# Attention passes of a two-layer transformer kernel: pieces of other work in the odd half sub-steps alone, two together

## The chip, the cores and the metric

One core of a Trainium2 chip. The metric is device microseconds of one execution; three runs of the kernel before are given. TensorE (PE) multiplies, VectorE (DVE), ScalarE (ACT) and GpSimd (POOL) do the rest, SyncE (SP) issues the DMAs. Each engine works through its own instructions in order, and waits on semaphores that others raise.

## The reference

For 4 batches of 512 tokens of 256 numbers (two layers, each an attention and a feed-forward part, each followed by a layer norm):

```python
x = L0_attn_hidden_states                         # (4, 512, 256)
x = _layernorm(x + _L0_attn_ref(x, ...))          # linear attention, 16 heads of 128, elu + 1
x = _layernorm(x + _L0_ffn_ref(x, ...))           # 8 low-rank updates, the one with the largest gate is taken
x = _layernorm(x + _L1_attn_ref(x, ...))          # below
x = _layernorm(x + _L1_ffn_ref(x, ...))           # 8 experts, the best 2, gated, plus a low-rank part

def _L1_attn_ref(x, Wq, Wk, Wv, Wo, bo):          # 16 heads of 16
    ...
    logits = jnp.einsum('bhqd,bhkd->bhqk', q, k) / jnp.sqrt(jnp.float32(hd))
    weights = jax.nn.softmax(logits, axis=-1)
    ctx = jnp.einsum('bhqk,bhkd->bhqd', weights, v)
    ctx = jnp.transpose(ctx, (0, 1, 3, 2)).reshape(B, T, D)
    return ctx @ Wo + bo
```

## The kernel before, in words

The first layer's attention runs first (some 350 us, untouched). Then come four passes over the batches, b = 0 to 3: pass b does the softmax attention of batch b, and in between it pieces of the other parts of neighbouring batches: for b+1 the update of layer 0's feed-forward part (`update`), its norm, the transposes `turn_x2`, `query_key` and `value`; for b+2 `turn_x1`, `select` and the gate's selection (`gate_...`); for b-1 `out_project`, its norm, `turn_x3`, `route`, the experts (`expert_up`, `expert_gate`, `turn_hidden`); for b-2 `expert_out` and the last norm. `more` is b+1 < 4, `most` b+2 < 4, `back` b > 0, `back2` b > 1.

A pass has 16 sub-steps (a group of 4 heads by a tile of 128 keys), each in two half steps, n = 0 to 31. In each half step, called step n from here on, TensorE does a *pair*: two transposed scores (`turned_score`, L1179, into bank_st) and, on other rows of the array, two plain scores of eight sub-steps ahead (`score`, L1158, into bank_s). ScalarE turns each transposed score into probabilities (`exponentials`, L1505), VectorE takes the maximum over the keys of each plain score (`maxima`, L1759). bank_s and bank_st have two buffers each. In even steps TensorE adds the *context* of the sub-step before (`context`, L1192, 8 matmuls into bank_c). Behind that it issues a piece of other work. The order on each engine is written out by hand: the lists of `if n == ...` in the three functions `body(b)` of TensorE (L1300), ScalarE (L1539) and VectorE (L1865). Nothing but semaphores ties the three lists together.

Two waits matter most:

```python
def score(b, h, t):
    u = 4 * h + t
    at_least(pe, max_ready, 64 * b + u - 1)      # the maximum of the score before last
def turned_score(b, s, j):
    at_least(pe, p_ready, 64 * b + u - 1)        # the exponential of the one before last
```

A third is on the banks of the pieces: side0 and side1 take the halves i = 0 and 1 of nearly all of them, and `take(i)` waits until what was last in the bank has been read (`last_read`), for example by `add_update` (L1741) after `update`, by `x2T_rest` (L1746) after `turn_x2`, by `qk_rest` (L1751) after `query_key`, by `add_attention` (L1786) after `out_project`. `query_key` waits besides for both halves of x2T_lo, `turn_x3` for x normalized by ScalarE (L1457).

The transposes of the context (`turn_context`, L1200) and of the maxima (`turn_max`, L1165), `route` and `turn_logits` go through a bank of their own, bank_t.

Of the kernel before, what the change touches and what calls it, by code (L numbers as in the profile page):

```python
# [17 lines left out]
B, T, D = 4, 512, 256  # L18
# [748 lines left out]
def update_attention_experts(nc, a, kept, out, first):  # L767
# [6 lines left out]
    with ExitStack() as ctx:  # L774
# [119 lines left out]
        def expert_half(b):  # L894

            return 20 if b + 1 < B else 16
# [167 lines left out]
        def _(pe):  # L1064
# [235 lines left out]
            def body(b):  # L1300
                more, most, back, back2 = b + 1 < B, b + 2 < B, b > 0, b > 1
                e = expert_half(b)
                for n in range(2 * SUBS):
# [18 lines left out]
                    if n in (12, 13) and more:  # L1322
                        value(b + 1, n - 12)
                    if n in (14, 15) and more:
                        query_key(b + 1, n - 12)
                    if n in (16, 17) and most:
                        turn_x1(b + 2, n - 16)
                    if n in (18, 19) and most:
                        select(b + 2, n - 18)
# [6 lines left out]
                    if n in (e + 9, e + 10, e + 11) and back:  # L1336
                        turn_hidden(b - 1, n - e - 9)
                    if n in (28, 29) and not more:
                        expert_out(b - 1, n - 28)
# [3 lines left out]
                    if n == 4:  # L1343
                        turn_max(b, 1)
# [4 lines left out]
                    if n == 13 and back:  # L1349
                        route(b - 1)  # L1350
                    if n == 14 and back:
                        turn_logits(b - 1)
# [99 lines left out]
        def _(act):  # L1452
# [86 lines left out]
            def body(b):  # L1539
                more, most, back, back2 = b + 1 < B, b + 2 < B, b > 0, b > 1  # L1540
                e = expert_half(b)
                for n in range(2 * SUBS):
# [15 lines left out]
                    if n in (10, 11) and back:  # L1558
                        x3T_out(b - 1, n - 10)
                    if n in (11, 19):  # L1560
                        shift_out(b, n // 8 + 1)
                    if n in (12, 13) and more:
                        value_out(b + 1, n - 12)
                    if n == 13 and back:
                        lgT_out(b - 1)
                    if n in (14, 15) and more:
                        qk_out(b + 1, n - 12)
                    if n in (16, 17) and most:
                        x1T_out(b + 2, n - 16)
                    if n == (16 if more else 15) and back:  # L1570
                        route_exp(b - 1)
                    if n in (17, 18) and most:
                        squares(b + 2, (0, 1) if n == 17 else (2, 3))
                    if n in (20, 21) and back2:
                        normalize(4, b - 2, xk[:, b % 2], (0, 1) if n == 20 else (2, 3))
                    if n in (e + 1, e + 3, e + 5, e + 7) and back:
# [7 lines left out]
                    if n in (e + 9, e + 10, e + 11) and back:  # L1584
                        hidden_out(b - 1, n - e - 9)
# [62 lines left out]
        def _(dve):  # L1648
# [216 lines left out]
            def body(b):  # L1865
                more, most, back, back2 = b + 1 < B, b + 2 < B, b > 0, b > 1
                e = expert_half(b)
                for n in range(2 * SUBS):
# [17 lines left out]
                    if b == 0 and n in (5, 28):  # L1886
                        residual_stats(2 + n // 28, range(NT))
                    if b == 0 and n in (6, 29):
                        residual_merge(2 + n // 29)
# [11 lines left out]
                    if n in (11, 12) and back:  # L1901
                        x3T_rest(b - 1, n - 11)
                    if n in (11, 12) and back2:
                        expert_stats(b - 2, n - 11)
                    if n in (13, 14) and most:
                        normalize_x1(b + 2, (0, 1) if n == 13 else (2, 3))
# [270 lines left out]
```

## Time and profile before

| | |
|---|---|
| median of 3 runs (757.58 to 768.87) | 761.38 us |
| the profiled execution | 755.98 us |
| its span | 754.1 us |
| TensorE busy | 701.9 us (93%) |
| VectorE busy | 506.9 us (67%) |
| ScalarE busy | 405.1 us (54%) |
| GpSimd busy | 108.6 us (14%) |
| chain that ended last | PE 71%, DVE 17%, ACT 4%, issue 4%, DMA 2% |
| maxima (L1759), 256 | 164.5 us busy, idle before them 58.5 |
| exponentials (L1505), 256 | 139.2 us busy, idle before them 66.5 |

Times in the rows are from the start of the span. A row is a group of instructions with its busy time; in brackets stands the idle time before it and what ended it. Matmuls overlap, so a busy TensorE may still be waiting in part: the length of a stretch tells more than its busy share. A row of a stretch reads: from:to, its length in us, then for each of PE, PEld (the weight loads of TensorE), DVE, ACT and POOL the busy us with the number of instructions, then the granted TensorE clock (1.00 is 2.4 GHz, 0.50 is 1.2 GHz, between them a mean over both), the DMA share and GB/s. The passes begin at 379.3, 457.5, 541.2 and 624.9 us.

### The profile page before, as it was taken

How to read it: one execution, taken by the hardware profiler on the slowest of the kernel's cores; microseconds unless marked ns; L12 is line 12 of the kernel's file. 1: busy time of each engine (PE TensorE's matmuls, PEld its weight loads, DVE VectorE, ACT ScalarE, POOL GpSimd, SP SyncE). 2: the span in 40 equal slices, each digit the busy share in tenths (PEclk: the TensorE clock that was granted, in tenths of full speed). 3: DMA queues.
4: the chain of work that ended last, by engine and by line, in shares of the span. 5: the costliest groups of instructions: out<-in, count | busy, mean ns of one | idle time of the engine just before them, and what ended most of it. 6: DMA issues, size and time to landing. Idle time of an engine off the chain costs nothing.

```text
span 754.1 us, 11354 instructions
## 1 busy us (share of the span) xinstructions
PE 701.9 (93%) x4038; PEld 481.4 (64%) x4038; DVE 506.9 (67%) x1129; ACT 405.1 (54%) x746; POOL 108.6 (14%) x107
## 2 busy tenths in 40 slices
PE   8899999999999999997899988999999999999685
PEld 5678987798779887895344634555455455355364
DVE  4566556765577566856767697969878885862351
ACT  5475356644664466443036764866656664656411
POOL 0302320132013421343001000200001000000100
PEclk9999999999999999998559999999999999899867
DMA  8300000010000020008604810373007700000000
GB/s 336 139 1 1 29 1 2 0 46 0 0 0 11 0 80 1 3 14 97 97 2 58 96 20 1 46 90 36 3 1 85 86 30 1 3 2 28 29 1 28
DMA packets 13996, 28.30 MB, mean 38 GB/s; under 512 B 2612, under 2 KB 3452, under 8 KB 13820
## 3 DMA queue, kind: packets, MB, share of 16 engines
q1 hardware_dynamic: 13948, 27.68, 19.9%
q8 instruction: 28, 0.46, 0.3%
q14 instruction: 20, 0.16, 0.1%
HBM read 12.60 MB, written 2.10 MB: 19 GB/s over the span
## 4 chain that ended last, share of the span: by engine, by line
PE 71%; DVE 17%; ACT 4%; issue 4%; DMA 2%; POOL 1%; SPq 0%; DVEq 0%; ACTq 0%; POOLq 0%
PE bank_y L414 11%; PE bank_q L355 10%; PE bank_st L1179 8%; DVE nmax L1759 7%; PE bank_c L1192 6%; PE bank_a L297 5%; PE side L1127 3%; PE bank_a L385 3%; PE side L1251 3%; PE bank_s L1158 3%; PE side L1282 2%; PE bank_a L331 2%; PE bank_n L370 2%; PE bank_q L397 2%; PE side L1211 2%
## 5 line engine op out<-in xcount | busy, mean ns | idle before, releaser
L1759 DVE TENSOR_REDUCE nmax<-bank_s 128x1 f32<-128x512 f32 x256 | 164.5, 685 | 58.5 <-PE bank_s L1158 57.3
L1505 ACT ACTIVATE shared<-bank_st 128x512 f32<-128x512 f32 x256 | 139.2, 596 | 66.5 <-PE bank_st L1179 65.8
L1158 PE MATMUL bank_s<-ks,qs 48*128 48x512 f32 x256 | 114.7, 509 | 7.9 <-DVE nmax L1759 6.2
L1179 PE MATMUL bank_st<-qs,ks 50*128 50x512 f32 x256 | 102.1, 469 | 4.3 <-ACT shared L1505 4.1
L615 DVE SCALAR_TENSOR_TENSOR sq<-bank_q,bq,eq 128x512 f32<-128x512 f32 x64 | 47.5, 744 | 47.8 <-ACT eq L498 47.8
L414 PE MATMUL bank_y<-m_hi,s_lo 128*128 128x256 f32 x256 | 73.2, 286 | 3.2 <-POOL s_lo L249 3.1
L1192 PE MATMUL bank_c<-shared,v 128*32 128x512 f32 x512 | 73.0, 644 | 0.9 <-ACT shared L1505 0.9
L1179 PEld LDWEIGHTS bank_st<-qs,ks 50*128 50x128 f32 x256 | 41.5, 192 | 50.4 <-issue 23.9
L414 PE MATMUL bank_y<-m_hi,s_hi 128*128 128x256 f32 x256 | 72.1, 282 | 0.0
L414 PE MATMUL bank_y<-m_lo,s_hi 128*128 128x256 f32 x256 | 72.1, 282 | 0.0
L249 POOL TENSOR_TENSOR s_lo<-sq,s_hi 128x512 fp32r<-128x512 f32 x32 | 42.8, 1337 | 187.2 <-ACT s_hi L503 187.2
L1158 PEld LDWEIGHTS bank_s<-ks,qs 48*128 48x128 f32 x256 | 46.2, 202 | 29.9 <-DVE nmax L1759 27.9
L503 ACT ACTIVATE s_hi<-sq 128x512 fp32r<-128x512 f32 x64 | 40.3, 631 | 44.2 <-DVE sq L632 44.2
L496 ACT ACTIVATE eq<-bank_q,bq_neg 128x512 f32<-128x512 f32 x64 | 43.8, 685 | 28.9 <-PE bank_q L355 28.1
L632 DVE TENSOR_TENSOR sq<-sq,bank_q 128x512 f32<-128x512 f32 x64 | 43.4, 684 | 23.4 <-PE bank_q L397 23.2
L355 PE MATMUL bank_q<-xT_hi,wq_lo 128*128 128x512 f32 x128 | 54.7, 428 | 3.8 <-DVE wq_lo L587 2.5
L414 PEld LDWEIGHTS bank_y<-m_hi,s_lo 128*128 128x128 f32 x256 | 48.2, 188 | 5.9 <-issue 3.5
L355 PE MATMUL bank_q<-xT_hi,wq_hi 128*128 128x512 f32 x128 | 50.5, 394 | 0.0
L355 PE MATMUL bank_q<-xT_lo,wq_hi 128*128 128x512 f32 x128 | 50.4, 394 | 0.0
L1002 POOL TENSOR_TENSOR ln_rstd<-ln_var,half 128x4 f32<-128x4 f32 x12 | 12.1, 1011 | 264.6 <-DVE ln_var L119 264.6
L414 PEld LDWEIGHTS bank_y<-m_lo,s_hi 128*128 128x128 f32 x256 | 48.2, 188 | 0.2
L414 PEld LDWEIGHTS bank_y<-m_hi,s_hi 128*128 128x128 f32 x256 | 48.2, 188 | 0.0
(264 smaller groups left out, 1330.3 us busy)
## 6 DMA issues: line engine op xcount, KB each, us to landing
qs<-qk_hi SPq DMA_DIRECT2D x16, 256.0 KB, 5.6
ks<-qk_hi SPq DMA_DIRECT2D x16, 256.0 KB, 10.3
xT<-in_xT SPq DMA_DIRECT2D x4, 512.0 KB, 4.7
sq<-in_wqT SPq DMA_DIRECT2D x2, 1024.0 KB, 9.4
wo<-in_woT SPq DMA_DIRECT2D x1, 2048.0 KB, 13.3
xs<-in_x SPq DMA_DIRECT2D x1, 2048.0 KB, 18.1
qs<-qk_lo SPq DMA_DIRECT2D x8, 256.0 KB, 7.8
ks<-qk_lo SPq DMA_DIRECT2D x8, 256.0 KB, 11.0
```

The lines of the kernel that those rows point to most:

```text
L249: pool.tensor_tensor(s_lo[:, n % 3, :], sq[:, n, :], s_hi[:, n % 3, :].bitcast(F32), ALU.subtract).then_inc(s_lo_ready[1], 1)
L355: mm = pe.matmul(q_bank("query", n)[:, :], lhs, rhs, start=i == 0, stop=i == 3 * KD - 1)
L414: mm = pe.matmul(bank_y4[:, t, :], lhs, rhs, start=n == 0 and i == 0 and t % 2 == 0, stop=n == H0 - 1 and i == 2, skip_group_check=True)
L496: act.activation(eq[:, n % 3, :], q_bank("query", n)[:, :], ACT.Relu, bias=bq_neg[:, h:h + 1], scale=-1.0).then_inc(eq_capped, 1)
L503: act.activation(s_hi[:, n % 3, :], sq[:, n, :], ACT.Copy).then_inc(s_hi_ready, 1)
L615: dve.scalar_tensor_tensor(out=sq[:, n, :], in0=q_bank("query", n)[:, :], scalar=bq1[:, h:h + 1], in1=eq[:, n % 3, :], op0=ALU.add, op1=AL ...
L632: dve.tensor_tensor(sq[:, n, :], sq[:, n, :], q_bank("factor", n)[:, :], ALU.mult).then_inc(scaled, 1)
L1158: pe.matmul(bank_s[u % 2][:, :], qs[part, b % 2, slot, t * P:(t + 1) * P], ks[part, b % 2, slot, :], start=True, stop=True).then_inc(s_don ...
L1179: pe.matmul(bank_st[u % 2][:, :], ks[part, b % 2, slot, kt * P:(kt + 1) * P], qs[part, b % 2, slot, :], start=True, stop=True).then_inc(st ...
L1192: mm = pe.matmul(bank_c[32 * j:32 * j + 32, :], v[:, b % 2, kt, 4 * g + j, :], probs[:, (4 * s + j) % SLOTS, :], start=kt == 0, stop=kt == 3)
L1505: act.activation(probs[:, u % SLOTS, :], bank_st[u % 2][:, :], ACT.Exp, scale=SCALE1).then_inc(p_ready, 1)
L1759: dve.tensor_reduce(nmax[:, g, t, j:j + 1], bank_s[u % 2][:, :], AX.X, ALU.max, negate=True).then_inc(max_ready, 1)
```

## The change

On TensorE every piece of an even step goes to the odd step after it, so that the two halves of a piece (i = 0 and 1) are issued one behind the other there; the even steps keep the pair and the context. `route` and `turn_logits` go one step later (14 and 15), the experts begin one step later (21, or 17 in the last pass), each tile's `expert_up` and `expert_gate` together in one odd step. On ScalarE and VectorE the parts that belong to the pieces follow: on VectorE mostly both halves together in the even step after. No operation is added or left out; only the order changes. The core of the diff (`e` is `expert_half(b)`):

```diff
-            return 20 if b + 1 < B else 16
+            return 21 if b + 1 < B else 17
@@ TensorE, body(b)
-                    if n < 2 and more:
-                        update(b + 1, n)
-                    if n in (2, 3) and back2:
-                        expert_out(b - 2, n - 2)
-                    if n in (4, 5) and back:
-                        out_project(b - 1, n - 4)
-                    if n in (6, 7) and more:
-                        turn_x2(b + 1, n - 6)
-                    if n in (8, 9) and more:
-                        query_key(b + 1, n - 8)
-                    if n in (10, 11) and back:
-                        turn_x3(b - 1, n - 10)
-                    if n in (12, 13) and more:
-                        value(b + 1, n - 12)
+                    if n == 1 and more:
+                        for i in range(2):
+                            update(b + 1, i)
+                    if n == 3 and back2:
+                        for i in range(2):
+                            expert_out(b - 2, i)
+                    if n == 5 and back:
+                        for i in range(2):
+                            out_project(b - 1, i)
+                    if n == 7 and more:
+                        for i in range(2):
+                            turn_x2(b + 1, i)
+                    if n == 9 and more:
+                        for i in range(2):
+                            query_key(b + 1, i)
...
                     if n in (e, e + 2, e + 4, e + 6) and back:
                         expert_up(b - 1, (n - e) // 2)
-                    if n in (e + 1, e + 3, e + 5, e + 7) and back:
                         expert_gate(b - 1, (n - e) // 2)
+                    if n == e + 8 and back:
+                        turn_hidden(b - 1, 0)
+                        turn_hidden(b - 1, 1)
+                    if n == e + 10 and back:
+                        turn_hidden(b - 1, 2)
...
-                    if n == 4:
+                    if n == (3 if b else 4):
                         turn_max(b, 1)
@@ ScalarE, body(b)
-                    if n in (6, 7) and more:
-                        x2T_out(b + 1, n - 6)
-                    if n in (8, 9) and more:
-                        qk_out(b + 1, n - 8)
+                    if n in (7, 8) and more:
+                        x2T_out(b + 1, n - 7)
+                    if n in (9, 10) and more:
+                        qk_out(b + 1, n - 9)
...
-                    if n == 9 and back:
+                    if n == 10 and back:
                         normalize(3, b - 1, xk[:, (b - 1) % 2])
@@ VectorE, body(b)
-                    if n in (1, 2) and more:
-                        add_update(b + 1, n - 1)
-                    if n in (3, 4) and back2:
-                        add_experts(b - 2, n - 3)
-                    if n in (3, 4) and more:
-                        update_stats(b + 1, (0, 1) if n == 3 else (2, 3))
-                    if n == 4 and more:
+                    if n == 2 and more:
+                        add_update(b + 1, 0)
+                        add_update(b + 1, 1)
+                    if n == 3 and more:
+                        update_stats(b + 1, range(NT))
                         merge(2, b + 1)
-                    if n in (5, 6) and back:
-                        add_attention(b - 1, n - 5)
+                    if n == 4 and back2:
+                        add_experts(b - 2, 0)
+                        add_experts(b - 2, 1)
+                    if n == 6 and back:
+                        add_attention(b - 1, 0)
+                        add_attention(b - 1, 1)
                     if n in (6, 7) and back:
                         attention_stats(b - 1, n - 6)
-                    if n == 7 and more:
+                    if n == 7 and back:
+                        merge(3, b - 1)
+                    if n == 8 and more:
                         x2T_rest(b + 1, 0)
                         x2T_rest(b + 1, 1)
-                    if n == 8 and back:
-                        merge(3, b - 1)
-                    if n in (9, 10) and more:
-                        qk_rest(b + 1, n - 9)
+                    if n == 10 and more:
+                        qk_rest(b + 1, 0)
+                        qk_rest(b + 1, 1)
...
-                    if n in (15, 16) and more:
-                        qk_rest(b + 1, n - 13)
-                    if n == 15 and back:
+                    if n == 16 and back:
                         route_rel(b - 1)
+                    if n == 16 and more:
+                        qk_rest(b + 1, 2)
+                        qk_rest(b + 1, 3)
                     if n == 16:
                         split_maxima(b, 3)
-                    if n == (17 if more else 16) and back:
+                    if n == 17 and back:
                         route_scores(b - 1)
-                    if n == (18 if more else 16) and back:
                         route_first(b - 1)
-                    if n == (19 if more else 16) and back:
+                    if n == (19 if more else 17) and back:
                         route_less(b - 1)
-                    if n == (20 if more else 17) and back:
                         route_second(b - 1)
...
                     if n in (e + 1, e + 3, e + 5, e + 7) and back:
                         weighted_up(b - 1, (n - e) // 2)
-                    if n in (e + 2, e + 4, e + 6, e + 8) and back:
-                        hidden(b - 1, (n - e) // 2 - 1)
+                        hidden(b - 1, (n - e) // 2)
```

Left out of it by the same pattern: TensorE's `turn_x3` (11), `value` (13), `query_key` 2 and 3 (15), `turn_x1` (17), `select` (19), `expert_out` of the last pass (29); ScalarE's `x3T_out` (11, 12), `value_out` (13, 14), `qk_out` 2 and 3 (15, 16), `tanh` (e, e+2, ...), `hidden_out` (e+9 and e+10); VectorE's `x3T_rest` (12), `expert_stats` (11), `normalize_x1` (13), `projections` (20), the gate's distances and inverse (21).

## Rows read from the trace of the kernel before

**Rows 1.** Stretches, passes 1 and 2 (columns: see the profile before).

```profile
457.54:541.15 83.61, 79.40 (x479) 43.58 (x479) 70.69 (x183) 53.61 (x111) 5.84 (x9) 1.00 0.33 39
541.15:624.89 83.74, 81.48 (x475) 44.78 (x475) 68.57 (x171) 52.72 (x104) 6.01 (x7) 1.00 0.35 46
```

**Rows 2.** Chain of work that ended last, pass 2: start, us, what.

```profile
548.05 2.79 PE side L1282 x12
...
555.94 1.93 PE side L1211 x8
...
567.07 1.60 PE side L1127 x6
...
600.30 0.91 PE side L1251 x6
...
601.87 1.25 PE side L1251 x6
```

**Rows 3.** Stretches as in rows 1: steps 6, 7 and 8 of pass 3.

```profile
643.05:644.72 1.67, 1.67 (x15) 0.46 (x14) 1.10 (x2) 1.07 (x2) 0.00 (x0) 1.00 0.01 4
644.72:645.99 1.27, 0.75 (x9) 0.46 (x5) 1.27 (x4) 0.76 (x3) 0.00 (x0) 1.00 0.00 0
645.99:649.77 3.78, 3.31 (x12) 0.72 (x12) 3.71 (x12) 1.53 (x3) 0.00 (x0) 0.73 0.00 0
```

**Rows 4.** Timeline, VectorE, pass 2, steps 6 to 8: start, us, engine, line, operation.

```profile
561.39 1.29 DVE L1759 TENSOR_REDUCE nmax<-bank_s 128x1 f32<-128x512 f32 x2 [0.70 <-PE bank_s L1158]
562.60 0.68 DVE L1786 TENSOR_TENSOR xk<-side,xs 128x512 f32<-128x512 f32 x1
563.19 0.74 DVE L1717 BATCH_NORM_STATS2 ln_bn<-xk 128x6 f32<-128x256 f32 x2
563.86 1.27 DVE L1759 TENSOR_REDUCE nmax<-bank_s 128x1 f32<-128x512 f32 x2
...
568.09 0.15 DVE L115 TENSOR_TENSOR ln_tmp<-ln_bn 128x4 f32<-128x4 f32 x1
...
568.62 0.17 DVE L119 SCALAR_TENSOR_TENSOR ln_var<-ln_tmp 128x4 f32<-128x4 f32 x1
```

**Rows 5.** Timeline, TensorE, pass 2, step 8: the start of query_key.

```profile
567.07 0.47 PE L1127 MATMUL side<-x2T_hi,wqkv_lo 128*128 128x512 f32 x1 [0.41 <-DVE x2T_lo L1746]
```

**Rows 6.** Timeline, VectorE, pass 1, steps 2 and 3.

```profile
464.59 0.25 DVE L1775 RECIPROCAL rsum<-bank_t 128x16 f32<-128x16 f32 x1
...
465.40 0.86 DVE L1741 SCALAR_TENSOR_TENSOR xf<-xf,keep,side 128x256 f32<-128x256 f32 x2
466.18 1.28 DVE L1759 TENSOR_REDUCE nmax<-bank_s 128x1 f32<-128x512 f32 x2
```

**Rows 7.** Stretches: 1/2-5, 2/6-15, 2/16-21, 1/16-21, 1/22-27, 0/0-7 (pass/steps).

```profile
462.81:473.89 11.08, 9.78 (x53) 5.12 (x53) 9.57 (x27) 5.84 (x12) 1.21 (x2) 1.00 0.01 2
560.82:589.83 29.01, 28.14 (x169) 15.50 (x168) 23.14 (x53) 19.36 (x39) 4.79 (x5) 1.00 0.52 64
589.83:603.04 13.21, 12.40 (x69) 5.75 (x68) 12.55 (x41) 9.46 (x19) 0.00 (x0) 1.00 0.95 103
502.91:516.98 14.07, 13.50 (x95) 7.76 (x94) 13.34 (x43) 10.60 (x26) 0.00 (x0) 1.00 0.89 96
516.98:532.55 15.57, 14.81 (x95) 8.60 (x94) 14.85 (x44) 8.71 (x18) 0.00 (x0) 1.00 0.01 2
379.34:400.67 21.33, 20.50 (x77) 8.56 (x76) 16.07 (x42) 11.13 (x22) 1.75 (x3) 0.63 0.01 2
```

**Rows 8.** Timeline, ScalarE, pass 2: the normalization ahead of turn_x3.

```profile
571.47 2.06 ACT L1457 ACTIVATE xk<-xk,ln_shift,ln_rstd 128x256 f32<-128x256 f32 x4
```

**Rows 9.** Timeline, VectorE, pass 2: maxima of steps 17, 20 and 21.

```profile
592.49 1.28 DVE L1759 TENSOR_REDUCE nmax<-bank_s 128x1 f32<-128x512 f32 x2
...
599.33 1.29 DVE L1759 TENSOR_REDUCE nmax<-bank_s 128x1 f32<-128x512 f32 x2
...
601.71 1.29 DVE L1759 TENSOR_REDUCE nmax<-bank_s 128x1 f32<-128x512 f32 x2
```

More of the change, by code:

```diff
@@ new lines, in body @@
+                    if n == 11 and back:
+                        for i in range(2):
+                            turn_x3(b - 1, i)
+                    if n == 13 and more:
+                        for i in range(2):
+                            value(b + 1, i)
+                    if n == 15 and more:
+                        for i in (2, 3):
+                            query_key(b + 1, i)
+                    if n == 17 and most:
+                        for i in range(2):
+                            turn_x1(b + 2, i)
@@ L1330, in body @@
+                    if n == 19 and most:
+                        for i in range(2):
+                            select(b + 2, i)
                     if n in (e, e + 2, e + 4, e + 6) and back:
                         expert_up(b - 1, (n - e) // 2)
-                    if n in (e + 1, e + 3, e + 5, e + 7) and back:
                         expert_gate(b - 1, (n - e) // 2)
+                    if n == e + 8 and back:
+                        turn_hidden(b - 1, 0)
+                        turn_hidden(b - 1, 1)
@@ L1334, in body @@
+                    if n == e + 10 and back:
+                        turn_hidden(b - 1, 2)
                     if n == 30 and most:
                         turn_hm(b + 2)
[L1336 to L1339, printed above, removed]
+                    if n == 29 and not more:
+                        for i in range(2):
+                            expert_out(b - 1, i)
@@ L1348, in body @@
                         turn_max(b, n // 8 + 1)
-                    if n == 13 and back:
+                    if n == 14 and back:
                         route(b - 1)
-                    if n == 14 and back:
+                    if n == 15 and back:
                         turn_logits(b - 1)
@@ L1583, in body @@
                         hmT_out(b + 2)
-                    if n in (e + 9, e + 10, e + 11) and back:
-                        hidden_out(b - 1, n - e - 9)
+                    if n == e + 9 and back:
+                        hidden_out(b - 1, 0)
+                        hidden_out(b - 1, 1)
+                    if n == e + 10 and back:
+                        hidden_out(b - 1, 2)
             def split_weights(i, n0, n1, hi):
@@ L1900, in body @@
                         context_out(b, n // 8 - 1)
[L1901 to L1906, printed above, removed]
-                    if n == 14 and back2:
+                    if n == 10 and more:
+                        qk_rest(b + 1, 0)
+                        qk_rest(b + 1, 1)
@@ L1908, in body @@
+                    if n == 11 and back2:
+                        expert_stats(b - 2, 0)
+                        expert_stats(b - 2, 1)
+                    if n == 12 and back:
+                        x3T_rest(b - 1, 0)
+                        x3T_rest(b - 1, 1)
+                    if n == 13 and most:
+                        normalize_x1(b + 2)
+                    if n == 15 and back2:
                         merge(4, b - 2)
-                    if n in (15, 16) and more:
-                        qk_rest(b + 1, n - 13)
@@ L1918, in body @@
                         route_first(b - 1)
-                    if n == (19 if more else 16) and back:
+                    if n == (19 if more else 17) and back:
                         route_less(b - 1)
-                    if n == (20 if more else 17) and back:
                         route_second(b - 1)
-                    if n in (19, 20) and most:
-                        projections(b + 2, n - 19)
+                    if n == 20 and most:
+                        projections(b + 2, 0)
+                        projections(b + 2, 1)
@@ L1940, in body @@
                         gate_pick(b + 2)
-                    if n in (29, 30) and not more:
-                        add_experts(b - 1, n - 29)
+                    if n == 30 and not more:
+                        add_experts(b - 1, 0)
+                        add_experts(b - 1, 1)
                     if n == 31 and not more:
```

45 lines of the change are left out of this document (19 added, 26 removed).

## The prediction

> **What bounds the kernel now.** I read the passes first, as stretches [rows 1]: passes 1 and 2 take 83.6 and 83.7 us of the 754. TensorE shows busy for 95% and 97% of them at a granted clock of 1.00 (2.4 GHz), VectorE for 70.7 and 68.6 us. So TensorE sets the time while it has pieces to do, and VectorE where it has not. The chain inside pass 2 [rows 2] gives the prices of the pieces: expert-out 2.79 us, output projection 1.93, query/key piece 1.60, expert-up 0.91, expert-gate 1.25. An even step with a pair and a context alone takes 1.66, and the pair of an odd one keeps TensorE some 0.7 [rows 3]. VectorE's rows [rows 4], start to start: two maxima 1.21 us, a 512-wide subtraction or addition 0.60, two statistics 0.67, a merge 0.70; then a context_out 0.81 and an update 0.78 [rows 6].
>
> The rule that ties the engines is in the code: the first score of a half step waits for the first maximum of the half step before, the second score for the second maximum, and the context and the pieces stand behind them in the same queue. If VectorE begins the maxima of step n at M, TensorE gets past the pair of step n+1 no earlier than M + 1.29 + 0.43 (the maxima's length, and a score). A test on the kernel before: from the maxima at 561.39 VectorE's queue is 1.21 + 0.60 + 0.67 + 1.21 + 0.67 + 1.20 (two x2T_rest) = 5.56, so query_key can begin at 566.95; it begins at 567.07 and waited for just that [rows 4, 5].
>
> **What the change does to TensorE's own sum: nothing.** The pieces are the same; with p for a piece, an even and an odd step cost 1.66 + p + 0.66 + p before and 1.66 + 0.66 + 2p after. An odd step without a piece takes 1.27 [rows 3], and about as many stay empty. What moves is VectorE's and ScalarE's work: both halves of each step of it now come together, after a long odd step in which VectorE had only its two maxima to do, and in front of the maxima that the next pairs need. I walk through the places by the rule above; times count from the start of the step named.
>
> **Pass 1, steps 2 to 5.** Step 2: maxima at 0.57, context_out 0.81 and now both updates, 2 x 0.78: done at 4.2. The maxima of step 3 start there, then all four statistics 1.33 and the merge 0.70: 7.45. Step 3 is nearly empty on TensorE; the pair of step 4 gets through at 4.2 + 1.72 = 5.9, its context ends at 6.95. The pair of step 5 needs the maxima begun at 7.45: 9.2. Two output projections, 3.86: 13.05. Before, 11.08 [rows 7]. **+2.0.** (Before, the second statistics and the merge lay under the projection of step 4.)
>
> **Pass 2, the same steps.** Expert-out in step 3 needs bank side0, free only after update 0 at 3.4; TensorE is there at 2.3: 1.1 of stall. The output projections wait 0.1 for add_experts, and 0.1 more is lost at a pair. **+1.3.** In pass 3 there is no update: **+0.3.**
>
> **Steps 6 to 15, passes 1 and 2.** From step 6: maxima at 0.57, both add_attention 1.20, statistics 0.67: 3.65. Maxima of step 7 there, statistics 0.67, merge 0.70: 6.2. Maxima of step 8: 7.4; both x2T_rest: 8.65. TensorE would be at query_key, now behind the pair of step 9, at 5.9 by its own work. Two pieces 3.20 and a transpose 0.44: step 10 starts at 12.3. In step 10 ScalarE has the exponentials, a qk_out and then the normalization of four tiles, 2.06 us [rows 8], so the second half of turn_x3 starts at 4.35 of step 10, where 2.9 would do; the x3T evictions behind it make value wait 0.1 more. Steps 10 to 13 take 11.4, steps 14 and 15, with the route product and turn_logits, 7.95. Together 31.65; before 29.0 [rows 7]. **+2.65 in each.** Pass 0 has no add_attention and no x3: **+0.3.** In pass 3 the pair of step 9 waits in the same way, where the kernel before had a slow clock: taken as 0.
>
> **Steps 16 to 21.** VectorE now has route_rel and both qk_rest in step 16, where half of that lay in step 15 under a query/key piece, and route_second ahead of the maxima of step 20. Measured [rows 9]: from the maxima of step 17 to those of step 20 6.84 us, with a context_out, route_scores, first and less; from there to those of 21 another 2.38, so route_second is 1.17. After: maxima of 17 at 3.8 of step 16 (before 2.66), those of 20 at 3.8 + 6.84 + 1.17 = 11.8, the pair of 21 through at 13.5, up and gate 2.16: 15.7. Before 13.2 with the same expert pieces [rows 7]. **+2.5 in pass 2.** In pass 1 the transposes of x1 and the selection fill part of it: 15.75 against 14.05 [rows 7], **+1.7.** In pass 0 both wait for qk_rest: **+1.0.**
>
> **The expert steps and the end.** Up, gate, pair, context: 4.48 for a tile, as before; weighted_up and hidden (about 1.5) fit under the even step plus up. In pass 1 the gate's selection loads VectorE too; I find 14.65 for steps 22 to 27, before 15.57 [rows 7]: **-0.9.** The last hidden waits for the tanh of step 27, so turn_hidden stalls 0.9 as it does now; **+0.4** in pass 1. The DMAs are the same issues: SyncE's stack loads wait for qk_lo of piece 1, which comes at 3.8 of step 10, 15.6 before step 16 needs it. GpSimd gets one merge earlier and holds nobody.
>
> **Pass 0.** Its first steps run at a granted 0.63 [rows 7], so at 1.2 GHz for most of it; both updates in step 1, update, statistics and merge in steps 2 and 3 against the same pairs: I find 23.0 for steps 0 to 7, before 21.3: **+1.7**. Projections in one step: **+0.7** for the rest.
>
> **Sum.** Pass 0: 1.7 + 0.3 + 1.0 + 0.7 = 3.7. Pass 1: 2.0 + 2.65 + 1.7 - 0.9 + 0.4 = 5.85. Pass 2: 1.3 + 2.65 + 2.5 = 6.45. Pass 3: 0.3. In all +16. The profiled execution has a span of 754.1 and took 756.0; with 16 it would take 772. The median of the three runs is 761.4, 5.4 above it, so 777 there.
>
> **The clock.** In step 7 of pass 3 TensorE is busy 0.75 of 1.27 us, and in step 8 the granted clock falls to 0.73 on the mean, so to 1.2 GHz within it [rows 3]. The thin stretch of steps 16 to 20 gets some 2.5 us longer, so a drop or two more are likely, at 1 to 3 us each (in step 8 the slowed context takes 1.9 where 1.0 would do). The sum leaves them out, the range holds two or three. The Trainium skill, page "TensorE: Matmul & The Clock Gate", section "Why this matters for your kernels", asks only that there be no long idle gap between bursts of matmuls. By that rule no drop would be added and the sum stays; the drop in step 8 follows idle times of about half a microsecond, which speaks against leaning on it.
>
> **Rivals.** *A, the stalls are partly taken back:* a late step lets the other engines get ahead, and my terms are worked out place by place, each from engines without arrears. If a third to two thirds go, +5 to +11: 766 to 772. For it: in pass 2 VectorE's queue of 5.56 us ahead of query_key was empty one step later. *B, the clock falls for tens of us,* as at pass 0's start: +9 to +20 more, 786 to 797. Against it: from step 21 on every odd step is full. *C, the other side, the free even steps win:* by the prices [rows 2, 3] the steps 16 to 21 of pass 2 need 10 of their 13.2 us, the steps 6 to 15 some 26.8 of 29.0; those waits, 5 us in a pass, are there to be gained. With half of them gone from passes 1 and 2: -5, 756. It decides if both x2T_rest are done before TensorE passes the pair of step 9, at 5.9 of step 6; by the queue it is 8.65. *D, nothing measurable,* if VectorE's order costs what the waits save: 757 to 765.
>
> **How the numbers follow.** Forecast 0.56, its own range 772 to 785; A 0.22; B 0.10; C 0.05; D 0.07. The line at 2%, about what a measurement of this kernel can tell from no change, is at 776.6. Three quarters of the forecast lie above it, since the clock can only add: 0.42 and 0.10 of B make 0.52 slower. The rest, 0.14, with A, D and 0.02 of C gives 0.45; 0.03 faster. The range 764 to 790 leaves out C, most of D and half of B.
>
> **What would show it.** Right: passes 1 and 2 at 89 to 90 us each; query_key in step 9 waiting for x2T_lo by 2 to 3 us; step 3 of pass 2 waiting for an update; more idle time on TensorE behind nmax. Wrong: passes of 84 us or less, or a difference that is in the granted clock alone. What would make it wrong: an order in VectorE's queue that I misread, since every term hangs on it, or arrears that cover each other.

## The result and the profile after

The changed kernel takes 777.54 us (776.82 to 778.02, 4 runs) where the kernel before takes 759.93 (757.58 to 768.87, 4 runs): a ratio of 1.0245, interval 1.0217 to 1.0273. By the medians it is slower by 17.6 us. Ratios and intervals, here and below, compare fast runs with fast runs and so can differ a little from the quotient of the medians. The profiled execution of after took 777.21 us with a span of 774.7, at a mean granted clock of 0.927; before, 755.98, 754.1 and 0.943.

The page of after: engines, granted clock over 40 slices, shares of the chain, groups (busy time, mean ns; idle time before them and what ended it).

```profile
span 774.7 us, 11346 instructions
PE 711.0 (92%) x4038; PEld 490.8 (63%) x4038; DVE 503.7 (65%) x1129; ACT 406.5 (52%) x746; POOL 108.5 (14%) x107
...
PEclk9999999999999999997578987999999899999967
...
PE 68%; DVE 19%; ACT 6%; issue 4%; POOL 1%; DMA 1%; DVEq 0%; ACTq 0%; SPq 0%; POOLq 0%
...
L1776 DVE TENSOR_REDUCE nmax<-bank_s 128x1 f32<-128x512 f32 x256 | 164.5, 683 | 81.7 <-PE bank_s L1158 80.9
L1519 ACT ACTIVATE shared<-bank_st 128x512 f32<-128x512 f32 x256 | 140.1, 595 | 97.0 <-PE bank_st L1179 95.5
...
L1158 PE MATMUL bank_s<-ks,qs 48*128 48x512 f32 x256 | 117.7, 522 | 10.3 <-DVE nmax L1776 7.9
...
L1158 PEld LDWEIGHTS bank_s<-ks,qs 48*128 48x128 f32 x256 | 49.0, 206 | 36.7 <-DVE nmax L1776 34.9
```

The work is the same (maxima 164.5 us, exponentials 140.1), the waiting is not. VectorE idles 81.7 us in front of its maxima where it idled 58.5, ScalarE 97.0 in front of the exponentials where it idled 66.5, and the profile puts both down to TensorE. TensorE's scores in turn wait for the maxima: the scores themselves 7.9 us where it was 6.2, the weight loads in front of them 34.9 where it was 27.9. So this is a ring that turns more slowly, not one engine with more to do.

Stretches of after, columns as in [rows 1] and [rows 7]: passes 1 and 2, then (pass/steps) 1/2-5, 2/2-5, 2/6-15, 2/16-21, 1/16-21, 1/22-27, 0/0-7, and 2/6-9; below them 1/0-1.

```profile
458.09:553.79 95.70, 87.84 (x478) 48.78 (x479) 70.24 (x184) 54.01 (x111) 6.74 (x10) 0.91 0.27 35
553.79:644.88 91.09, 83.76 (x474) 47.52 (x475) 66.80 (x170) 53.28 (x104) 5.99 (x7) 0.94 0.31 42
466.65:481.46 14.81, 13.67 (x53) 6.86 (x52) 9.27 (x26) 6.98 (x13) 1.21 (x2) 0.76 0.01 2
558.63:574.23 15.60, 14.23 (x77) 9.56 (x77) 10.46 (x28) 6.75 (x13) 1.22 (x2) 1.00 0.01 2
574.23:606.97 32.74, 30.05 (x167) 17.11 (x166) 22.04 (x53) 18.81 (x36) 4.77 (x5) 0.95 0.41 51
606.97:622.80 15.83, 14.39 (x69) 6.09 (x68) 13.01 (x40) 10.35 (x20) 0.00 (x0) 0.78 0.81 97
513.74:529.66 15.92, 14.35 (x93) 8.09 (x92) 14.52 (x46) 10.52 (x26) 0.00 (x0) 1.00 0.80 96
529.66:544.84 15.18, 14.54 (x93) 8.82 (x92) 14.17 (x42) 8.60 (x18) 0.00 (x0) 1.00 0.01 2
379.00:401.01 22.01, 20.60 (x77) 9.20 (x76) 16.45 (x42) 11.62 (x22) 2.14 (x3) 0.63 0.01 2
574.23:587.92 13.69, 12.36 (x57) 6.80 (x56) 9.56 (x23) 6.63 (x12) 3.56 (x3) 0.88 0.00 1
...
458.09:466.65 8.56, 8.52 (x28) 4.62 (x28) 3.79 (x8) 3.11 (x6) 0.92 (x1) 0.61 0.01 2
```

Two stretches of before that the rows ahead do not have, 2/2-5 and 2/6-9:

```profile
546.29:560.79 14.50, 14.50 (x77) 9.12 (x76) 10.98 (x29) 5.71 (x12) 1.22 (x2) 1.00 0.00 1
560.79:571.27 10.48, 10.05 (x57) 5.37 (x56) 9.42 (x22) 7.42 (x16) 2.33 (x3) 1.00 0.06 11
```

The loss lies in passes 1 and 2: 95.70 and 91.09 us against 83.61 and 83.74 [rows 1]. Pass 0 adds 0.9, pass 3 with the end 0.6. In pass 1 the first two steps have 3.3 us of the 12.1 (8.56 for 5.27, at a granted clock of 0.61): a place to which the prediction gave nothing. The column of the granted clock, the last but two, is under 1.00 in all but three of the stretches of passes 1 and 2; in the same stretches of before it was 1.00 throughout. After the long low stretch at pass 0's start (37.5 us, in both kernels) TensorE is at 1.2 GHz for 41 us in the passes of after, in short stretches of 3.4 to 10.2 us, and for 13.7 us in those of before. The second profile of the same kernel (below) has its low stretches in part elsewhere: there passes 1 and 2 take 93.22 and 90.06 us, and the first two steps of pass 1 5.46 at full clock.

The place that the prediction worked out most closely, VectorE's timeline in steps 6 to 8 of pass 2 and TensorE's first matmul of query_key, now in step 9:

```profile
574.80 1.29 DVE L1776 TENSOR_REDUCE nmax<-bank_s 128x1 f32<-128x512 f32 x2 [2.54 <-PE bank_s L1158]
576.00 1.28 DVE L1803 TENSOR_TENSOR xk<-side,xs 128x512 f32<-128x512 f32 x2
577.20 0.74 DVE L1734 BATCH_NORM_STATS2 ln_bn<-xk 128x6 f32<-128x256 f32 x2
577.86 1.27 DVE L1776 TENSOR_REDUCE nmax<-bank_s 128x1 f32<-128x512 f32 x2
579.05 0.74 DVE L1734 BATCH_NORM_STATS2 ln_bn<-xk 128x6 f32<-128x256 f32 x2
579.82 0.17 DVE L115 TENSOR_TENSOR ln_tmp<-ln_bn 128x4 f32<-128x4 f32 x1
...
580.46 1.28 DVE L1776 TENSOR_REDUCE nmax<-bank_s 128x1 f32<-128x512 f32 x2
581.66 1.27 DVE L1763 TENSOR_TENSOR x2T_lo<-side,x2T_hi 128x512 fp32r<-128x512 f32 x2
```

```profile
583.03 0.76 PE L1127 MATMUL side<-x2T_hi,wqkv_lo 128*128 128x512 f32 x1 [0.75 <-DVE x2T_lo L1763]
```

VectorE first idles 2.54 us while TensorE is in its long odd step. Then it works without a gap: the maxima of step 6, both add_attention, two statistics, the maxima of step 7, two statistics, the merge, the maxima of step 8 and both x2T_rest, for which query_key waits. From the maxima of step 6 to query_key it is 8.23 us; it was 5.68 [rows 4, 5], and the queue as counted ahead gives 8.08.

### The profile page after: what moved, and what is told of

Read it like the earlier page. It is cut to its first block, busy times and chain, and to the rows that moved or that the text cites. A ratio compares the mean times of both kernels' runs of the same rounds, so it can differ in the third digit from the quotient of the medians.

```text
span 774.7 us, 11346 instructions
## 1 busy us (share of the span) xinstructions
PE 711.0 (92%) x4038; PEld 490.8 (63%) x4038; DVE 503.7 (65%) x1129; ACT 406.5 (52%) x746; POOL 108.5 (14%) x107
## 4 chain that ended last, share of the span: by engine, by line
PE 68%; DVE 19%; ACT 6%; issue 4%; POOL 1%; DMA 1%; DVEq 0%; ACTq 0%; SPq 0%; POOLq 0%
PE bank_y L414 10%; PE bank_q L355 10%; DVE nmax L1776 8%; PE bank_st L1179 6%; PE bank_c L1192 5%; PE bank_a L297 4%; PE side L1127 3%; PE bank_s L1158 3%; PE bank_a L385 3%; PE side L1251 2%; PE side L1282 2%; PE bank_a L331 2%; PE side L1141 2%; PE bank_n L370 2%; PE side L1211 2%
## 5 line engine op out<-in xcount | busy, mean ns | idle before, releaser
L1776 DVE TENSOR_REDUCE nmax<-bank_s 128x1 f32<-128x512 f32 x256 | 164.5, 683 | 81.7 <-PE bank_s L1158 80.9
L1519 ACT ACTIVATE shared<-bank_st 128x512 f32<-128x512 f32 x256 | 140.1, 595 | 97.0 <-PE bank_st L1179 95.5
L1158 PE MATMUL bank_s<-ks,qs 48*128 48x512 f32 x256 | 117.7, 522 | 10.3 <-DVE nmax L1776 7.9
L1179 PE MATMUL bank_st<-qs,ks 50*128 50x512 f32 x256 | 106.4, 482 | 4.8 <-ACT shared L1519 4.8
L1158 PEld LDWEIGHTS bank_s<-ks,qs 48*128 48x128 f32 x256 | 49.0, 206 | 36.7 <-DVE nmax L1776 34.9
L1002 POOL TENSOR_TENSOR ln_rstd<-ln_var,half 128x4 f32<-128x4 f32 x12 | 12.1, 1011 | 273.8 <-DVE ln_var L119 273.8
```

What stands on the lines that cost most here:

```text
L1158: pe.matmul(bank_s[u % 2][:, :], qs[part, b % 2, slot, t * P:(t + 1) * P], ks[part, b % 2, slot, :], start=True, stop=True).then_inc(s_don ...
L1179: pe.matmul(bank_st[u % 2][:, :], ks[part, b % 2, slot, kt * P:(kt + 1) * P], qs[part, b % 2, slot, :], start=True, stop=True).then_inc(st ...
L1519: act.activation(probs[:, u % SLOTS, :], bank_st[u % 2][:, :], ACT.Exp, scale=SCALE1).then_inc(p_ready, 1)
L1776: dve.tensor_reduce(nmax[:, g, t, j:j + 1], bank_s[u % 2][:, :], AX.X, ALU.max, negate=True).then_inc(max_ready, 1)
```

## The experiments

**All of VectorE's early parts a step forward, TensorE as in the change.** This is not the order of before, since TensorE issues both halves of a piece in the odd step: the second half of an addition comes a step earlier than there, the second x2T_rest a step later. The theory says that the loss is VectorE's order, the rival that it is TensorE's pairing or the clock.

```diff
 VectorE: add_update, both halves             n 2 -> 1
          update_stats                        all in 3 -> (0, 1) in 3, (2, 3) in 4;  merge(2)  3 -> 4
          add_experts, both                   n 4 -> 3
          add_attention, both                 n 6 -> 5
          x2T_rest                            both in 8 -> 7 and 8;  merge(3)  7 -> 8
```

> TensorE's order is that of the kernel after; only VectorE's order is changed, in steps 1 to 8: both updates in step 1, statistics in 3 and 4 with the merge in 4, both add_experts in 3, both add_attention in 5, x2T_rest in 7 and 8 with the merge behind it. Theory V (the loss is VectorE's late order): steps 2 to 5 of pass 1 lose some 3 us against the kernel after, steps 6 to 9 some 2 us in passes 1 and 2; in all -7 to -9, so about 769 where the kernel after has 777.5. Theory T (two pieces together starve the other engines, whatever VectorE's order): within 2 us of 777.5. Theory C (the clock alone): within 3 us at equal low time, the wait of query_key for x2T_lo gone without any gain in the time.

Measured: 759.17 against 758.91, ratio 1.0001 (0.9959 to 1.0043). The direction is that of theory V, but 18 us came back where it had 7 to 9. Pass 1 as a whole and its steps 2-5 and 6-9, then pass 3:

```profile
460.26:544.61 84.35, 78.28 (x478) 44.37 (x479) 70.20 (x184) 53.34 (x111) 6.83 (x10) 1.00 0.31 39
465.72:475.57 9.85, 9.44 (x53) 5.24 (x52) 8.79 (x25) 6.10 (x12) 1.21 (x2) 1.00 0.01 2
475.57:485.93 10.36, 10.12 (x57) 5.65 (x56) 8.78 (x22) 6.96 (x14) 2.67 (x3) 1.00 0.01 2
...
630.89:704.44 73.55, 71.46 (x397) 39.22 (x398) 43.37 (x124) 45.23 (x90) 2.41 (x4) 1.00 0.02 9
```

In the total the whole loss is gone, and the steps 2 to 5 are even shorter than before (9.85 against 11.08 [rows 7]; both updates are now done before the maxima of step 2, so nothing but the context's part stands between these and those of step 3. That this is why was not tried by itself). So in sum the pairing of pieces on TensorE costs nothing by itself. By place it is a balance, though: in pass 1 the steps 14 and 15 and 16 to 21 are still at 7.77 and 15.93 us (before: 6.48 and 14.07), and the steps 2 to 5 and 10 to 13 gain nearly as much (9.85 and 10.82 for 11.08 and 12.06). Passes 1 and 2 are 0.7 and 2.5 us longer than in the profile of before, pass 0 1.8; pass 3 is 3.3 shorter, and there the kernel before had 6.8 us of low clock and this run none. Most of the low clock in passes 1 and 2 went with the waits (none in pass 1, 6.8 us in pass 2), though nothing on TensorE was moved.

**VectorE's late parts back alone, and both together.**

```diff
 VectorE: qk_rest(2), (3)    both in 16 -> 15 and 16
          route_rel          16 -> 15
          route_second       19 -> 20 (where there is a next batch)
```

> The kernel after with VectorE's order in steps 15 to 20 put back: qk_rest 2 and route_rel in step 15, route_second behind the maxima of step 20. Theory V: steps 16 to 21 of pass 2 go from 15.8 to about 13.6 us, those of pass 1 from 15.8 to about 14.5; in all -3 to -4, so about 774. Theory T: no change, 777. Theory C: no change where the clock is equal.

> Both changes of VectorE's order together, TensorE's order that of the kernel after. Theory V: the gains add, -10 to -13, about 765 to 768, that is within 1% of the kernel before. Theory T: 775 or more. Theory C: the time follows the low time of the clock and not the waits: if some 40 us of the passes stay at 1.2 GHz, 770 or more.

Measured: 777.51 against 758.91, 1.0194 (1.0123 to 1.0266), for the late parts alone; with the early ones too 759.98, 0.9987 (0.9943 to 1.003). The late parts bring nothing: the steps 16 to 21 of pass 1 take 16.42 us where they took 15.92. With both, the total is that of before again, where 765 to 768 was expected. Stretch, then VectorE and ScalarE in pass 2, late parts alone:

```profile
514.71:531.13 16.42, 14.39 (x93) 8.08 (x92) 13.55 (x43) 10.54 (x26) 0.00 (x0) 1.00 0.82 93
```

```profile
613.77 0.69 DVE L1768 TENSOR_TENSOR qk_lo<-side,qk_hi 128x512 fp32r<-128x512 f32 x1 [1.06 <-ACT qk_hi L1504]
```

```profile
611.44 1.09 ACT L1519 ACTIVATE shared<-bank_st 128x512 f32<-128x512 f32 x2 [2.23 <-PE bank_st L1179]
612.65 0.60 ACT L1529 ACTIVATE ctT<-bank_c 128x512 f32<-128x512 f32 x1
613.14 0.59 ACT L1504 ACTIVATE qk_hi<-side 128x512 fp32r<-128x512 f32 x1
```

The expectation for the late parts fell. VectorE stands 1.06 us in front of qk_rest(3), which needs ScalarE's qk_out(3); and that is queued in step 16 behind the exponentials and a context's eviction. One list put back leaves the work tied to the other.

**The late part of the change alone:** the kernel before up to step 12, the changed one from step 13.

> The change from step 13 on alone; the first thirteen steps of each pass have the order of the kernel before, on all engines. If the places add (the sum of the prediction: +1.0, +1.7 and +2.5 in steps 16 to 21, -0.9 and +0.4 around the experts), +4 to +5 us over the kernel before, 763 to 765 where it has 759, with steps 16 to 21 at 12.9, 15.9 and 15.5 to 15.8 us. If instead the whole loss comes from the first steps (the early order of VectorE gave all of it back), within 2 us of the kernel before.

Measured: 764.27 against 759.46, 1.0107 (1.0054 to 1.016). Steps 16 to 21 of passes 0, 1 and 2:

```profile
422.75:435.69 12.94, 11.72 (x82) 6.12 (x81) 9.92 (x23) 9.99 (x25) 0.00 (x0) 1.00 0.96 113
506.24:522.17 15.93, 14.37 (x95) 8.08 (x94) 14.56 (x46) 10.53 (x26) 0.00 (x0) 1.00 0.81 96
595.31:610.81 15.50, 14.29 (x71) 6.11 (x70) 13.01 (x40) 10.25 (x20) 0.00 (x0) 0.78 0.83 99
```

The three lengths fit the prediction's 12.8, 15.75 and 15.7, the third with a granted clock of 0.78 in it. The late part makes some 5 of the 18 us, as expected. It does not simply add to the early part, which by the first experiment is worth all 18: with VectorE early, gains elsewhere cover the late steps.

**ScalarE's list early too.** On top of the two edits of VectorE:

```diff
 ScalarE: qk_out(2), (3)     15 and 16 -> both in 15;  normalize(3)  10 -> 9
 VectorE: qk_rest(2), (3)    15 and 16 -> both in 15
          x2T_rest(0) and merge(3) in 7, x2T_rest(1) in 8
```

> TensorE's order is that of the kernel after; VectorE's as in the run with both changes, and ScalarE's too: the normalization for turn_x3 in step 9 ahead of qk_out, qk_out 2 and 3 both in step 15 and both qk_rest there. Theory V': in steps 16 to 21 the second qk_rest had waited for ScalarE's qk_out behind the exponentials and context_out of step 16; with it early the maxima of step 17 start 1 us sooner, steps 16 to 21 of pass 1 go from 16.4 to about 15.2 us and steps 10 to 13 from 10.8 to about 10: 3 to 5 us under the run before it at equal low time of the clock, 755 to 757. Rival (VectorE's own sum of work sets steps 16 to 21): no change there beyond 0.4 us.

Measured: 755.97 against 759.46, 0.9974 (0.9944 to 1.0004), as expected. Steps 16 to 21 of passes 1 and 2, then the same in the run with both edits of VectorE alone:

```profile
506.22:521.06 14.84, 14.02 (x93) 7.95 (x92) 13.17 (x43) 10.02 (x25) 0.00 (x0) 1.00 0.91 103
595.96:608.75 12.79, 11.83 (x69) 5.57 (x68) 12.05 (x39) 9.54 (x19) 0.00 (x0) 1.00 1.04 119
```

```profile
507.37:523.80 16.43, 14.38 (x94) 8.07 (x93) 13.55 (x43) 10.54 (x26) 0.00 (x0) 1.00 0.82 93
596.54:614.17 17.63, 15.97 (x70) 7.33 (x69) 12.51 (x39) 10.36 (x20) 0.00 (x0) 0.72 0.81 105
```

Both edits of VectorE alone had left 16.43 and, with 10 us of low clock in it, 17.63; before it is 14.07 and 13.21 [rows 7]. Which of the moves here does it, the last group settles: there qk_out and qk_rest 2 and 3 are all that moves beside both edits of VectorE, and the lengths are 14.84 and 12.81. So qk_out(3) on ScalarE, with the qk_rest(3) that waits for it, held the steps 16 to 21; the two moved together, and ScalarE's was not moved with VectorE's late order left as in the change.

**One number.** The changed kernel with `if n == 6 and back: add_attention` made `if n == 5`, and the changed kernel once more beside it.

> The kernel after with one number changed: both add_attention in step 5, where VectorE waits anyway, instead of step 6. Theory V: VectorE's queue ahead of query_key is 1.2 us shorter, so steps 6 to 9 of passes 1 and 2 take 11.0 us at the full clock where they took 12.2; with pass 3 2.5 to 3.5 us less in all, 774 to 775. Rival (the queue is not what holds query_key): steps 6 to 9 stay at 12.2 or, with a low stretch, at 13.7.

> The kernel after once more, to set its spans beside the low time of the clock as for the kernel before (whose spans grow by 0.31 us for each us of low time, 40 executions between 74 and 120 us). If waits and clock add, its spans lie 12 to 14 us above that line at equal low time, and its low time is 10 to 20 us above the 96 of the kernel before on the mean. If it is the clock alone, they lie on the line.

Measured: 772.06 against 758.68, 1.0163 (1.01 to 1.0226), and 776.82, 1.0248 (1.0186 to 1.031). Steps 6 to 9 of pass 2, first the changed kernel again, then with the one number:

```profile
571.17:583.32 12.15, 10.83 (x59) 5.66 (x58) 9.57 (x23) 6.62 (x12) 3.57 (x3) 1.00 0.01 1
```

```profile
575.11:586.23 11.12, 10.17 (x59) 5.64 (x58) 8.98 (x22) 6.30 (x12) 3.57 (x3) 1.00 0.01 1
```

Both at full clock, so this is waiting alone: 12.15 (the prediction had 12.3) and, with 1.20 us of VectorE's work taken out from between two pairs of maxima, 11.12 (11.0 was expected). The total gained 4.8 us where 2.5 to 3.5 were expected: between these two profiles pass 3 alone is 4.4 us shorter, and it has 10.2 us of low clock in the repeat and none here. The same steps of the same kernel took 13.69 in its first profile, where the clock was at 0.88: the 1.5 between them is what the low stretch cost there.

**Filling the waits of TensorE.** Is the low clock a cost of its own, which could be had back while the waits stay? Two further copies of each transposed score keep TensorE multiplying, in steps 4, 5, 7, 8, 9 and 17 to 20, then in 8, 9 and 18 to 20 alone.

```diff
             def turned_score(b, s, j, copies=0):
+                for _ in range(copies):
+                    pe.matmul(bank_st[u % 2] ...)        # the same operands, start=True
```

> The kernel after; in steps 4, 5, 7, 8, 9 and 17 to 20 of passes 1 to 3 each transposed score is issued three times into the same bank (the same result), to fill TensorE's waits: 108 matmuls more at 0.23 us, most of them inside waits. Theory C (thin stretches bring the clock down, and that is half of the loss): the low time in passes 1 to 3 falls from 34 us to under 15, the time by 2 to 8 us to 770 to 775. Rival (the waits are what costs, the clock only follows): low time may fall, the time stays at 777 or rises to 785, by the added matmuls that lie on the path.

> The kernel after; copies of the transposed scores only in steps 8, 9, 18, 19 and 20 of passes 1 to 3, where TensorE waits for VectorE (60 matmuls more). If low time costs 0.3 to 0.45 us for each us and the thin steps bring it: low time of the execution from 111 to about 95 us, and 773 to 775. If the earlier fill was no gain because the clock does not matter: 777 or more with the low time down.

Measured: 779.44 against 758.91, 1.0318 (1.0261 to 1.0375), and 777.13 against 759.46, 1.0246 (1.0193 to 1.0299). Both expectations of a gain fell (770 to 775 and 773 to 775). Steps 16-21 of pass 2 in the first, then steps 6-9 and 16-21 of pass 2 in the second:

```profile
603.51:618.99 15.48, 14.97 (x85) 8.08 (x84) 13.01 (x40) 10.35 (x20) 0.00 (x0) 1.00 0.84 101
```

```profile
574.84:587.01 12.17, 11.23 (x66) 6.91 (x66) 9.57 (x23) 6.80 (x12) 3.58 (x3) 1.00 0.01 1
606.08:625.96 19.88, 19.34 (x82) 9.71 (x82) 13.38 (x40) 10.46 (x20) 0.00 (x0) 0.66 0.64 77
```

The first has less time at the low clock than the change: 84, 92, 95 and 116 us in its four runs, where eight runs of the change have 107 to 119. But the copies lengthen the steps that they fill (steps 2 to 5 of pass 2 take 17.20 us where they took 15.60, both at full clock), and the total does not fall. The second has 99 to 110 us. In its profile the steps 6 to 9 kept the full clock at the length of the waits, but the steps 16 to 21 were at 1.2 GHz for 13.7 us, and the total is that of the change. What makes the clock fall was not found; with copies there was somewhat less low time on the mean, and low stretches all the same. That steps 6 to 9 had full clock in the repeat of the change too, without a copy, leaves even their case undecided.

**Three arrangements from the findings.** *Hybrid:* the experiment with ScalarE early, but the transposes of x1, the selection and the experts in all three lists where they were before. *Merge back:* both edits of VectorE, and qk_out and qk_rest 2 and 3 in step 15, the rest untouched. *Statistics behind:* that, and

```diff
 ScalarE: x2T_out             7 and 8 -> both in 7
 VectorE: attention_stats(1)  7 -> 8, behind the maxima of step 8
```

> The order of a3_scalar_early_too up to step 15, and from 16 on TensorE's pieces as in the kernel before (turn_x1 16 and 17, select 18 and 19, experts from 20, one product a step). If the places add: steps 0 to 9 0.5 to 1.4 us a pass shorter than in the kernel before, steps 16 to 21 as there (14.1 and 13.2): 3 to 5 us under it, 754 to 756. If the early pairing leaves arrears to the later steps: 759 or more.

> TensorE's order of the kernel after; VectorE and ScalarE do each piece's part in the odd step itself where the data allow (qk_out and qk_rest 2 and 3 in step 15), the merge for x3 stays behind the maxima of step 8 and the normalization in step 10. Steps 6 to 9 go back from 11.0 to 10.4, steps 16 to 21 stay at 14.8 and 12.8: 754.5 to 756, against 759.5 for the kernel before. Rival: what the early merge cost is paid back in steps 10 to 13, so 756 as a3_scalar_early_too.

> As a4_merge_back, with both x2T_out in step 7 and the second attention statistics behind the maxima of step 8: VectorE's queue ahead of query_key is 0.65 us shorter. Steps 6 to 9 at 9.9 to 10.0 us, 1 to 1.5 us under a4_merge_back in all. Rival (TensorE's own work of 9.6 us is reached, or ScalarE holds the pair of step 9): no gain over a4.

Measured: hybrid 759.0 against 759.46, 1.0019 (0.9991 to 1.0046); merge back 759.09 against 758.68, 0.9985 (0.9946 to 1.0024); statistics behind 754.5 against 758.68, 0.9975 (0.9939 to 1.0012). The hybrid was expected at 754 to 756 and merge back at 754.5 to 756: neither gained. Steps 6 to 9 of pass 2 in the last two:

```profile
570.49:580.83 10.34, 10.10 (x57) 5.64 (x56) 8.79 (x22) 6.95 (x14) 2.65 (x3) 1.00 0.00 0
```

```profile
560.55:570.29 9.74, 9.60 (x59) 5.58 (x58) 8.94 (x22) 6.93 (x14) 1.90 (x3) 1.00 0.00 0
```

9.74 is under the 10.48 of before: with x2T_rest ahead and the statistics behind, the even steps alone do give something. The last one's median is the lowest of all, but its interval reaches 1.0012, so it isn't shown to beat the kernel before. Its median is 4.6 us under that of merge back, where 1 to 1.5 were expected; most of that is the clock (next section).

## Why the prediction was right, and where it was not

**Where the 18 us lie.** Over 65 executions of the kernel before, the span follows the time at the low clock, L = 2 x (1 - granted clock) x span: span = 727.1 + 0.316 x L, with a scatter of 1.0 us (L from 74 to 120). Eight executions of after have a mean span of 775.1 with L = 112.6, before's mean is 757.5 with L = 96.2. The line gives 762.7 for 112.6, so 12.4 us are waiting at an equal clock and 16.4 x 0.316 = 5.2 are the clock. Without the ten longest executions the line is 729.8 + 0.286 x L, and the waits come to 13.2: the split is uncertain by about 1 us. By the line of all 65 all early parts forward leave 0.5 of the 12.4, the late parts alone 12.6, the one number 7.8, the late part of the change alone makes 2.2, the copies leave 21.0 and 14.7 (the copies' own time is in it); merge back and statistics behind lie 1.7 and 2.2 under it. So of the 4.6 us between the last two, 0.5 are left at an equal clock.

**The bound and the rule: right.** The span's loss hangs on VectorE's order, as the first experiment shows with TensorE's order left alone. The rule "maxima at M, next pair through at M + 1.72", and one queue added up, gave the start of query_key within 0.15 us. The wait there is 0.75 us, not the 2 to 3 forecast, because TensorE had its delay already at the pair of step 9. The prediction's own rule says so: it has the maxima of step 8 at 6.2, so the pair of step 9 through at 7.9 and not, as its forecast of the wait assumed, at TensorE's own 5.9; up to 8.65 that leaves 0.7. Expert-out in step 3 of pass 2 waits for the update as forecast, 1.19 us for 1.1:

```profile
562.22 1.10 PE L1282 MATMUL side<-down,turned 128*128 128x256 f32 x4 [1.19 <-DVE xf L1758]
```

**Steps 2 to 5.** Pass 2: 15.60 against 14.50 before, +1.1 for +1.3. Pass 1: 14.81 at a clock of 0.76; the 13.05 was seen in no run at full clock, so +2.0 is neither confirmed nor refuted.

**Steps 6 to 15.** At full clock 12.15 + 11.33 + 7.72 = 31.2 against 29.01: +2.2 for +2.65. Steps 6 to 9 give 1.7 of it, forecast 1.8; the rest, put down to ScalarE and the last steps, was overdrawn (0.5 for 0.85). Pass 1 got less: at full clock its steps 10 to 13 take 10.81 and its steps 14 and 15 7.72, where before took 12.06 and 6.48, so from step 10 on nothing was lost there, and with the 12.2 of both filling runs for the steps 6 to 9 the term is +1.7 for +2.65.

**Steps 16 to 21: the size right, the reason not whole.** 15.92 and 15.83 for 15.75 and 15.7. The 15.83 of pass 2 has 6.8 us of low clock in it (granted clock 0.78); the first filling run took 15.48 there at full clock, so the waits make +2.3 at most of the +2.5. I had put the delay on VectorE's own queue in steps 16 to 20. Putting that queue back gained nothing; with ScalarE's qk_out moved a step forward as well the steps came down. I had added up one queue where two were late. That they were late by about the same is how I read it; ScalarE's part was not moved alone.

**The rest.** Steps 22 to 27 of pass 1: 15.18, -0.4 for -0.9. Pass 0, steps 0 to 7: 22.01, +0.7 for +1.7; that the granted clock of 0.63 there stretches TensorE's side and hides more of VectorE's is likely, but was not tested. Its steps 16 to 21: 12.92 for 11.80, +1.1 for +1.0. Pass 3, steps 2 to 5: -0.1 for +0.3. Together the waits are 12.4 where the sum had 16.

**The clock.** It was left out of the sum and put at a drop or two. It was more: L rose by 16 us, though a microsecond of it cost only 0.32. This goes far to explain why passes 1 and 2 took 95.70 and 91.09 us (93.22 and 90.06 in the repeat) where the prediction's sign of being right was 89 to 90 for each. By the rule that the prediction quotes from the Trainium skill (page "TensorE: Matmul & The Clock Gate", section "Why this matters for your kernels") no drop would be added; the traces contradict that, for steps 6 to 9 of pass 2 have one while TensorE shows busy for 12.36 of 13.69 us, and no single wait of TensorE inside the passes is longer than 1.2 us.

**Luck in the number.** That the total came out at the forecast's 777 has three errors in it, which cancel: waits 3.6 too high, clock 5.2 too low, and a start from 761.4 where the median of before with a fourth run is 759.93, 1.5 too high.

**The rivals.** A (a part of the stalls taken back): by its size of 12.4 for 16 it happened to about a fifth, not a third. B (tens of microseconds of low clock in one stretch): no, short stretches, 5.2 us. C (the free even steps win): false for this order, but its bound, x2T_rest done before the pair of step 9, is what the last arrangement comes near to, with 9.74 in steps 6 to 9. D: shown false by the interval.

## What to carry to other kernels

In a ring of engines with orders written by hand, a piece moved on one engine costs nothing where the others' parts stand, in their own queues, behind nothing that the ring needs: add up each queue from one ring signal (here the maxima) to the next, for every engine that feeds the piece, not for the busiest alone. Group work that is ready at once, but put it in front of the signal only if the next consumer needs it. And price the clock from many executions of the same kernel, where low time and span can be set against each other.

## What the runs showed of the hardware

Over 65 executions of the kernel before, a microsecond of TensorE at 1.2 GHz goes with 0.32 us more of the span; 0.5 would be lost if TensorE alone set the time. That the rest falls under waits for other engines is the likely reason, and was not shown. Copies of matmuls that fill TensorE's waits did not keep the clock at 2.4 GHz: L was 84 to 116 us with copies in nine steps of a pass, 99 to 110 with copies in five, 107 to 119 with none.

A small VectorE operation can take ten times its time beside GpSimd. The copies of the maxima (128x16) of before and after: count, then least, median and greatest ns.

```profile
L1765 DVE CAST nmax_parts<-nmax x16: 165/165/1584, 366.2 to 666.7; 128x16 fp32r<-128x16 f32 x16
```

```profile
L1782 DVE CAST nmax_parts<-nmax x16: 162/164/238, 365.9 to 688.1; 128x16 fp32r<-128x16 f32 x16
```

Before has two of 1.58 us, in passes 1 and 2. The second in the timeline, and below it one of 2.46 us from the first experiment's run, a subtraction of the same size (median 175 ns):

```profile
570.11 2.41 POOL L1018 TENSOR_TENSOR xs<-xf,bo 128x1024 f32<-128x1024 f32 x1
570.98 1.58 DVE L1765 CAST nmax_parts<-nmax 128x16 fp32r<-128x16 f32 x1
```

```profile
572.44 2.43 POOL L1018 TENSOR_TENSOR xs<-xf,bo 128x1024 f32<-128x1024 f32 x1
```

```profile
572.44 2.46 DVE L1784 TENSOR_TENSOR nmax_parts<-nmax,nmax_parts 128x16 fp32r<-128x16 f32 x1
```

The copy ends at 572.56, GpSimd's addition at 572.52; the subtraction ends 0.03 us after its addition. The Trainium skill, page "SBUF — State Buffer", section "Who interferes with whom", says of the port pair that VectorE's copies and GpSimd share that it is a lock held for a whole instruction; this trace agrees, with 1.4 us of VectorE for one copy that starts at the wrong moment. What such a copy costs the kernel was not measured; while the first of the two ran, in pass 1, the chain that ended last went through ScalarE's qk_out and normalization.
